# Attention over pairs of heads on one core: an earlier swap of the first query's rotary halves, and new orders of a pair's four blocks on three engines

## What is computed

```python
def _L0_attn_ref(x, W_kvd, b_kvd, W_ku, b_ku, W_vu, b_vu, W_kr, b_kr, W_qd, b_qd, W_qu, b_qu, W_qr, b_qr, W_o, b_o):
    ...
    kv_c = x @ W_kvd + b_kvd
    keys_c = heads(kv_c @ W_ku + b_ku, HD)
    values = heads(kv_c @ W_vu + b_vu, HD)
    keys_r = _apply_rope(heads(kv_c @ W_kr + b_kr, RD))
    q_c = x @ W_qd + b_qd
    queries_c = heads(q_c @ W_qu + b_qu, HD)
    queries_r = _apply_rope(heads(q_c @ W_qr + b_qr, RD))
    ...
    scores = jnp.einsum('bhqd,bhkd->bhqk', q, k) * scale
    scores = jnp.where(causal[None, None], jnp.float32(-1000000000.0), scores)
    probs = jax.nn.softmax(scores, axis=-1)
    ctx = jnp.einsum('bhqk,bhkd->bhqd', probs, values)
    ...
xn = _layernorm(x, axis=-1)
x = x + attn(xn) + einsum('bsi,oi->bso', xn, binarized(weight)) + bias
```

## Time and profile before

| what | value |
|---|---|
| median of 3 runs | 1412.74 us (1407.88 to 1415.17) |
| the profiled execution | 1410.69 us, span in the trace 1408.9 us |
| TensorE matmuls, share of the span | 97% |
| ScalarE | 85% |
| VectorE | 81% |
| GpSimd | 71% |
| mean granted TensorE clock | 0.997 of full speed |

### The profile page before, as it was taken

How to read it: one execution, slowest core, us unless ns; L and a number is a source line. 1 busy time by engine, 2 the same in 40 slices (tenths; PEclk the granted TensorE clock), 3 DMA queues, 4 the chain that set the end, 5 groups by cost and what they waited for, 6 DMA issues and landing times.

```text
span 1408.9 us, 27603 instructions
## 1 busy us (share of the span) xinstructions
PE 1373.1 (97%) x9786; PEld 1229.7 (87%) x9786; DVE 1146.4 (81%) x2708; ACT 1200.5 (85%) x2603; POOL 1000.4 (71%) x573
## 2 busy tenths in 40 slices
PE   6979999999999999999999999999999999999998
PEld 4769999997898999888899999999789999999987
DVE  4858898885788888887688889888678888888898
ACT  4659889997788988998788999899878988889887
POOL 6986777777667777769666787777766877777750
PEclk9999999999999999999999999999999999999999
DMA  9851222212343322211333222222233322221110
GB/s 274 228 127 50 72 54 64 64 50 64 76 107 79 83 64 64 64 34 47 79 94 92 64 80 64 65 57 57 63 77 87 88 64 65 64 60 45 40 31 31
DMA packets 46957, 106.82 MB, mean 76 GB/s; under 512 B 9333, under 2 KB 17830, under 8 KB 46822
## 3 DMA queue, kind: packets, MB, share of 16 engines
q1 hardware_dynamic: 43360, 94.01, 26.0%
q0 software_dynamic: 3296, 11.01, 2.8%
q10 hardware_dynamic: 166, 0.03, 0.0%
HBM read 48.92 MB, written 9.96 MB: 42 GB/s over the span
## 4 chain that ended last, share of the span: by engine, by line
PE 79%; ACT 7%; POOL 5%; DVE 5%; DMA 2%; issue 1%; SPq 1%; POOLq 0%; ACTq 0%; DVEq 0%
PE ring L1509 11%; PE turn L1564 10%; PE u_ps L1585 9%; PE ring L1539 9%; PE ring L1540 8%; PE ring L1541 8%; PE u_ps L1586 8%; PE o_ps L1609 4%; PE o_ps L1610 4%; PE ring L1522 3%; ACT probs L788 2%; PE ring L1448 2%; PE ring L1454 2%; DVE probs L1086 1%; DVE probs_lo L1096 1%; POOL k_rope L377 1%
## 5 line engine op out<-in xcount | busy, mean ns | idle before, releaser
L1086 DVE TENSOR_SCALAR_CACHE_REDUCE probs<-ring,c_t 128x1024 f32<-128x1024 f32 (+7 forms) x512 | 413.2, 809 | 85.7 <-PE ring L1541 85.2
L1096 DVE TENSOR_TENSOR probs_lo<-turn,probs_hi 128x512 fp32r<-128x512 f32 (+1 forms) x640 | 401.0, 630 | 65.7 <-ACT probs_hi L797 61.0
L797 ACT ACTIVATE probs_hi<-turn 128x512 fp32r<-128x512 f32 (+1 forms) x640 | 346.4, 550 | 94.0 <-PE turn L1564 91.2
L788 ACT ACTIVATE probs<-probs,row_min 128x1024 f32<-128x1024 f32 (+7 forms) x512 | 394.5, 772 | 11.8 <-DVE probs L1086 9.5
L1564 PE MATMUL turn<-ident,probs_r 128*128 128x128 f32 x2304 | 315.9, 244 | 4.6 <-DVE probs_lo L1096 2.7
L1585 PE MATMUL u_ps<-probs_hi,kv_nat 128*128 128x256 f32 x1147 | 313.5, 301 | 1.2 <-DVE u_pair L1102 1.2
L1564 PEld LDWEIGHTS turn<-ident,probs_r 128*128 128x128 f32 x2304 | 267.9, 141 | 36.5 <-DVE probs_lo L1096 15.3
L1586 PE MATMUL u_ps<-probs_lo,kv_nat 128*128 128x256 f32 x1147 | 289.7, 281 | 0.0
L1539 PE MATMUL ring<-k_hi,q_hi 128*128 128x512 f32 (+3 forms) x768 | 273.6, 356 | 0.0
L1540 PE MATMUL ring<-k_lo,q_hi 128*128 128x512 f32 (+3 forms) x768 | 262.9, 342 | 0.0
L1541 PE MATMUL ring<-k_hi,q_lo 128*128 128x512 f32 (+3 forms) x768 | 262.7, 342 | 0.0
(11 more groups left out here) (229 smaller groups left out, 2585.8 us busy)
## 6 DMA issues: line engine op xcount, KB each, us to landing
swapped<-k_rope SPq DMA_DIRECT2D x128, 128.0 KB, 2.3
wv<-wv_scratch SPq DMA_DIRECT2D x62, 256.0 KB, 4.0
wp<-wp_scratch SPq DMA_DIRECT2D x62, 192.0 KB, 3.5
wp<-wp_scratch SPq DMA_DIRECT2D x31, 256.0 KB, 3.1
swapped<-q_y SPq DMA_DIRECT2D x62, 128.0 KB, 2.3
swapped<-q_x SPq DMA_DIRECT2D x62, 128.0 KB, 2.3
k_hi<-qb_kv_hi SPq DMA_DIRECT2D x16, 256.0 KB, 3.7
k_lo<-qb_kv_lo SPq DMA_DIRECT2D x16, 256.0 KB, 5.0
```

The lines of the kernel that those rows point to most:

```text
L788: act.activation(p, p, ACT.Exp, scale=-1.0, bias=row_min[:, r:r + 1], accum_out=row_sum[:, g % 4, w, h:h + 1]).then_inc(exp_ready, 1)
L797: act.activation(probs_hi[:, r % 4, 0:width], turn[r % 2][:, 0:width], ACT.Identity).then_inc(turned_hi, 1)
L1086: dve.tensor_scalar(probs_of(g, w, h), ring[slot_of(entry)][:, KEY_COLUMN[qt]:KEY_COLUMN[qt] + keys], c_t[b % 2][:, qt, ds(pair * 2 + h, 1 ...
L1096: dve.tensor_tensor(probs_lo[:, r % 4, 0:width], turn[r % 2][:, 0:width], probs_hi[:, r % 4, 0:width].bitcast(F32), ALU.subtract).then_inc ...
```

## The change

The swap of a pair's queries is split. `swap(m, 1)` waited until both queries were evacuated and then issued the second query's two DMAs and the first's. Now it waits for the first query alone, issues its two DMAs, then waits for the second query and issues the other two; the keys, the first and the second query each signal a semaphore of their own, and `rope` waits for the first query's at its step 3 and for the second's at step 4.

Masks are calls of their own and no longer stand inside a group of transposes. The last score of block 3 of a pair (`scores(g - 1, 3, 0)`) stands at the beginning of the next pair's block 0, its exponential too. All four blocks have new orders on TensorE, ScalarE and VectorE, and two entries of `NEXT_BATCH` move. No computing instruction is added or removed.

```diff
-NEXT_BATCH = {(5, 3, 0): (("transpose", 0),), (5, 3, 3): (("transpose", 1),), (6, 0, 3): (("down", 0),), (6, 1, 2): (("down", 1),),
-              (6, 2, 2): (("linear", 0),), (6, 3, 2): (("linear", 1),), (7, 3, 0): (("natural", 0),), (7, 3, 2): (("natural", 1),)}
+NEXT_BATCH = {(5, 2, 3): (("transpose", 0),),
...
+              (6, 3, 0): (("linear", 0),),
...
-                    engine.wait_ge(swap_done, swaps_done(m, 0) if m > 0 else 16 * SWAP_DMAS)
-                if n == 3 and m > 0:
-                    engine.wait_ge(swap_done, swaps_done(m, 1))
+                    engine.wait_ge(keys_swapped, 16 * SWAP_DMAS * (m + 1))
+                if n in (3, 4) and m > 0:
+                    engine.wait_ge((x_swapped, y_swapped)[n - 3], 16 * 2 * m)
...
                 else:
-                    sp.wait_ge(evacuated, m * PROJ_ITEMS + PROJ_ITEMS)
+                    sp.wait_ge(evacuated, m * PROJ_ITEMS + QUERY_X + 1)
 
                     sp.wait_ge(rope_step, m * ROPE_OPS + 3)
...
+                    swap_rows(64, q_x, x_swapped)
+                    sp.wait_ge(evacuated, m * PROJ_ITEMS + QUERY_Y + 1)
+                    swap_rows(0, q_y, y_swapped)
+                    return
+                swap_rows(0, k_rope, keys_swapped)
+                swap_rows(64, k_rope, keys_swapped)
```

ScalarE's new order of block 0 (the lines that are new or stand elsewhere have a +):

```diff
                     evacuate(g, ROPE_K)
                     turned_high(g - 1, 0)
-                    u_again(g - 2, 0)
                     u_high(g - 2, 1)
                     turned_high(g - 1, 1)
+                    u_again(g - 2, 0)
+                    exponent(g - 1, 3)
+                    if pair == 5:
+                        next_apply(b + 1, 1)
+                    u_again(g - 2, 1)
+                    turned_high(g - 1, 2)
+                    exponent(g, 0)
+                    exponent(g, 1)
+                    turned_high(g - 1, 3)
+                    turned_high(g - 1, 4)
+                    u_high(g - 1, 0)
+                    exponent(g, 2)
                     if pair == 4:
                         next_inverse(b + 1)
-                    turned_high(g - 1, 2)
-                    if pair == 5:
-                        next_apply(b + 1, 1)
-                    turned_high(g - 1, 3)
-                    exponent(g, 0)
-                    exponent(g, 1)
-                    u_high(g - 1, 0)
-                    u_again(g - 2, 1)
-                    exponent(g, 2)
-                    turned_high(g - 1, 4)
-                    u_again(g - 1, 0)
+                    evacuate(g, QUERY_X)
                     if pair == 6:
                         next_left("down", b + 1, 0)
-                    evacuate(g, QUERY_X)
                     turned_high(g, 0)
+                    u_again(g - 1, 0)
                     turned_high(g, 1)
```

TensorE's of the same block:

```diff
                 if n == 0:
+                    scores(g - 1, 3, 0)
                     project(g, ROPE_K)
                     output(g - 3, 1)
+                    weigh_group(g - 2, 3)
                     turn_group(g - 1, 0)
-                    turn_group(g - 1, 1, (g, 0))
-                    weigh_group(g - 2, 3)
+                    turn_group(g - 1, 1)
+                    mask(g, 0)
                     weigh_group(g - 2, 4)
                     head_ready(g, 0)
                     scores(g, 0, 0)
                     scores(g, 0, 1)
-                    turn_group(g - 1, 2, (g, 1))
+                    turn_group(g - 1, 2)
+                    mask(g, 1)
                     output(g - 2, 0)
                     weigh_group(g - 1, 0)
+                    scores(g, 1, 0)
                     weigh_group(g - 1, 1)
-                    scores(g, 1, 0)
-                    turn_group(g - 1, 3, (g, 2))
+                    turn_group(g - 1, 3)
+                    mask(g, 2)
...
                     output(g - 2, 1)
-                    turn_group(g, 0, (g, 3))
+                    turn_group(g, 0)
+                    mask(g, 3)
+                    scores(g, 3, 0)
                     weigh_group(g - 1, 3)
-                    scores(g, 3, 0)
-                    turn_group(g, 1, (g + 1, 0))
+                    turn_group(g, 1)
+                    mask(g + 1, 0)
```

In block 1 two masks now stand between other matmuls, in block 3 one; the output of block 3 stands behind the second score there:

```diff
                     output(g - 2, 0)
-                    turn_group(g - 1, 2, (g, 1))
+                    mask(g, 1)
                     weigh_group(g - 2, 4)
...
                     weigh_group(g - 1, 0)
+                    mask(g, 3)
+                    scores(g, 3, 0)
+                    output(g - 2, 1)
                     weigh_group(g - 1, 1)
-                    turn_group(g - 1, 4, (g, 3))
-                    output(g - 2, 1)
-                    scores(g, 3, 0)
+                    turn_group(g - 1, 4)
...
+                    mask(g, 1)
                     scores(g, 1, 0)
+                    output(g - 2, 0)
...
+                    mask(g, 2)
+                    weigh_group(g - 1, 0)
                     scores(g, 2, 0)
```

More of the change, by code:

```diff
@@ L392, in _, with swap_rows @@
         def _(sp):
+            def swap_rows(rows, source, signal):
+                for a, b in ((rows, rows + 32), (rows + 32, rows)):
+                    sp.dma_start(swapped[a:a + 32, :], source[b:b + 32, :]).then_inc(signal, 16)
             def swap(m, which):
@@ L400, in swap @@
                 else:
-                    sp.wait_ge(evacuated, m * PROJ_ITEMS + PROJ_ITEMS)
+                    sp.wait_ge(evacuated, m * PROJ_ITEMS + QUERY_X + 1)
                     sp.wait_ge(rope_step, m * ROPE_OPS + 3)
-                for rows, source in ((0, k_rope if which == 0 else q_y), (64, k_rope if which == 0 else q_x)):
-                    for a, b in ((rows, rows + 32), (rows + 32, rows)):
-                        sp.dma_start(swapped[a:a + 32, :], source[b:b + 32, :]).then_inc(swap_done, 16)
+                    swap_rows(64, q_x, x_swapped)
[4 more added lines that the diff above has]
+                swap_rows(64, k_rope, keys_swapped)
             def load_wp(m):
@@ L865, in sequence @@
                     u_high(g - 1, 1)
                     turned_high(g, 1)
-                    if not (pair == 6 and b + 1 < NB):
-                        turned_high(g, 2)
-                elif n == 2:
+                    turned_high(g, 2)
+                else:
                     exponent(g, 0)
-                    if pair == 6 and b + 1 < NB:
-                        turned_high(g - 1, 2)
-                    turned_high(g - 1, 3)
+                    high_queries(g, 1)
                     u_again(g - 2, 1)
```

229 lines of the change are left out of this document (119 added, 110 removed).

## The result

The changed kernel takes 1399.35 us (median of 4 runs, 1398.56 to 1401.42) against 1412.08 for the kernel before on the same chips: a ratio of 0.9914, 95% interval 0.9886 to 0.9942. The profiled execution took 1401.42 us, its span is 1399.4. Batches are counted from 0 here and in the expectations, so the prediction's second batch is batch 1.

What follows compares the result with a forecast made beforehand. TensorE's list of matmuls was taken to bound the kernel, with 1.17 us of short waits per plain pair. 5.2 - 13.9 - 5.4 - 0.8 - 1.8 = -16.7 us gave a forecast of 1395 us, range 1382 to 1416.

Steps and rivals of the forecast that it cites:

- Positions: TensorE's new order, mainly three masks per pair between other matmuls at 0.12 us: +0.18 a plain pair, +5.2 in all.
- The waits: TensorE's short waits for ScalarE and VectorE: 1.17 us falls to 0.35 per plain pair, -13.9 over seventeen pairs.
- the prediction's margins: Time in hand in a plain pair: 0.2 us at the transposes, 0.45 at the mask behind the first query.
- the slower rival: Key projection waits for VectorE's minimum once 0.4 us in hand is used up: up to 1428 us, chance 0.12.
- the 38.25 worked out: Length in us of a plain pair in the new order if TensorE's matmuls had nothing to wait for.
- the better case: Rival: the five tight places hold, or lone masks cost no more: 1384 us, chance 0.10.
- the two steps of ScalarE that the prediction singled out: Fourth exponential moved three steps behind, first query's evacuation moved earlier: TensorE's waits of 0.15 and 0.23 us go.
- Pair 5: Pair also preparing the next batch: waits fall from 1.8 to 0.95 us in each of three batches.
- Pair 6: New 1.65 us mask wait behind the "down" evacuation, most other waits gone: -0.8 us over three pairs.
- The swap: First query's DMAs issued earlier: rotary chain ends about 3.6 us earlier, buying nothing in a plain pair.
- pair 0's -1.8: Gain from the earlier swap in the second batch's pair 0, where ScalarE waited for GpSimd: -1.8 us.
- First pair: With last pair and drain, has waits the order hardly touches: 0, give or take 1.5 us.

Runs made afterwards that it cites:

- experiment 7: Changed kernel with ScalarE's fourth exponential of the block before put back ahead of the keys' evacuation: 1432.80 us, ratio 1.0164 to the kernel before.
- experiment 11: Changed kernel with ScalarE's first query evacuation put back behind the block's first high halves and a copy: 1440.00 us, ratio 1.0196 to the kernel before.
- experiment 4: Changed kernel with ScalarE taking pair 6's first down projection out of the ring before evacuating the first query: 1396.37 us, ratio 0.9903 to the kernel before.
- experiment 2: Kernel before with the split swap alone, all orders as before: 1418.52 us, ratio 1.0063 to the kernel before.
- experiment 1: Changed kernel with the queries' swap late again, both behind the second query's evacuation: 1406.05 us, ratio 0.9976 to the kernel before.
- experiment 8: Changed kernel with the queries' swap late and ScalarE's high halves of the queries two steps later: 1394.26 us, ratio 0.9887 to the kernel before.
- experiment 3: Changed kernel with GpSimd's first query product in pair 0 waiting for VectorE's low half of the values: 1392.99 us, ratio 0.9883 to the kernel before.
- experiment 12: Changed kernel with GpSimd behind the values, pair 6's down projection first, a store behind the keys' swap: 1382.81 us, ratio 0.9805 to the kernel before.
- experiment 9: Changed kernel with GpSimd behind the values, down projection first, pair 0's second query evacuation ahead of keys' high halves: 1391.34 us, ratio 0.9867 to the kernel before.

## Why the prediction held, and where it failed

The direction, the range and the mechanism of the orders were right; the gain was 12.7 us instead of 17. That it came so near is in part luck: in the table, terms that came out worse than forecast add up to some 14 us and terms that came out better to some 7.

*Positions.* A lone mask costs the 0.12 that was taken from the earlier trace rows. The Trainium skill, TensorE: Matmul & The Clock Gate, The mechanism, would have it cost nothing extra; the rows of the mask above decide otherwise.

*The waits.* What TensorE's weight loads waited for the named causes, over the whole run (us in total, times, longest us), before and now:

```profile
PEld turn L1564 <- DVE probs_lo L1096: 15.3, 36, 0.7
PEld turn L1564 <- ACT probs L788: 7.1, 29, 0.9
PEld ring L1522 <- ACT q_x L702: 3.8, 23, 0.2
...
PEld turn L1571 <- DVE probs_lo L1103: 3.0, 8, 1.0
PEld turn L1571 <- ACT probs L799: 3.6, 5, 1.8
```

The mask's wait for the first query is gone altogether. Two of the places in a plain pair, the transposes behind the first two scores and the mask behind the first query:

```profile
1159.54 0.69 DVE L1103 TENSOR_TENSOR probs_lo<-turn,probs_hi 128x512 fp32r<-128x512 f32 x1
...
1160.80 0.28 PE L1571 MATMUL turn<-ident,probs_r 128*128 128x128 f32 x2
...
1167.80 1.12 ACT L713 ACTIVATE q_x<-ring,bias_p 128x1024 f32<-128x1024 f32 x1 [0.36 <-PE ring L1516]
...
1169.61 0.23 PE L1529 MATMUL ring<-mask_bf,ident_bf 128*128 128x128 bf16 x1
```

The low halves end 0.57 us ahead of the transposes and the evacuation 0.69 ahead of the mask. So the prediction's margins were too small: some 0.5 and 0.6 us are in hand, not 0.2 and 0.45. The key projection that was to wait in the slower rival hardly does: 0.17 us in three plain pairs. 0.24 us are left on the 38.25 worked out, where 0.35 were allowed for: a third of the way from the forecast to the better case. (That rival's terms, all taken, come to 1381 and not to its 1384.) Experiments 7 and 11 show that the two steps of ScalarE that the prediction singled out are needed: each, put back alone, costs 1.2 us a plain pair, more than the 0.75 gained. How the 0.75 divides among the moves is not shown. Pair 5 (-4.0, not -2.0) and pair 7 (-1.0, not +0.5) were undersized too, and pair 4 oversized (-1.4, not -2.3).

*Pair 6.* A wait of 1.65 behind the "down" evacuation was forecast; 1.44 stand in the trace, and experiment 4 takes it away.

GpSimd's waits in a plain pair became what was forecast (the second was to be about 1 us):

```profile
1174.50 2.40 POOL L380 TENSOR_TENSOR q_x<-q_x,cos 64x1024 f32<-64x1024 f32 x1 [0.17 <-POOL k_lo L391]
1177.65 2.39 POOL L380 TENSOR_TENSOR q_y<-q_y,cos 64x1024 f32<-64x1024 f32 x1 [0.75 <-DMA swapped<-q_y]
```

*The swap* is the step that failed, in both halves. "In a plain pair that buys nothing" was read from the old orders, for which experiment 2 shows it true; in the new ones it is worth some 0.6 us in a plain pair (experiment 1), because ScalarE's high halves of the queries had moved ahead, which I had laid out without asking when GpSimd delivers them (experiment 8). And pair 0's -1.8 became a loss: batch 1 did fall, by 1.4, but in the other batches GpSimd's product, no longer held up, lies on VectorE's split of the values. I asked what waits for GpSimd's product and not what runs beside it. Experiments 2 and 3 show this from both sides. A part of the loss is the keys' late swap, which experiment 12 takes away.

*First pair.* Taken as 0, it lost 3.0, by the same collision: 41.99 with GpSimd behind the values. The mean granted clock of this pair was 0.85, before 0.92, so the lower level lasted some 14 us there instead of 7.

Open: in the changed kernel GpSimd began 8.0 us after the keys' evacuation in batch 2, 2.0 more than the usual 4.35 and the late start of 1.67 explain (of the swap's four DMAs the third landed at 5.2 us, the last at 7.9); and why the clock stands at its lower level for part of some prologues. The three traces with the longest ones (39.66, 38.27 and 37.27 us, of experiments 4, 11 and 9) have 10.2, 3.4 and 3.4 us of it; this blurs medians of 4 to 6 runs.

## What to carry to other kernels

When a step of one engine starts earlier, lay it beside what every other engine does in its new place, not only beside its readers: an idle stretch that is filled may have been what a neighbour's instruction ran in. Work that happens once per batch (a store, a split of values) meets an order that was laid out for plain steps; look at each queue's list at that boundary. The steps of an order hang together: two of them put back alone (experiments 7 and 11) each cost more than the whole change had gained, while a third (4) took away a wait that the prediction had priced, and gave 4.8 us in its trace. So look at each moved step against its neighbours on every engine.

## What the hardware showed that was not expected

VectorE's subtraction of two SBUF tiles (128x512) takes 0.69 us alone and, where it finds a GpSimd product running, ends about 0.55 us after that, 2.5 to 2.8 in all. It is the second to begin that pays: in experiment 4's batch 1 VectorE began 0.16 us ahead and took 0.69, and GpSimd's product took 2.79 instead of 2.40:

```profile
431.56 0.69 DVE L1080 TENSOR_TENSOR kv_nat<-xn,kv_nat 128x512 fp32r<-128x512 f32 x1
431.72 2.79 POOL L380 TENSOR_TENSOR q_x<-q_x,cos 64x1024 f32<-64x1024 f32 x1 [0.68 <-DMA swapped<-q_x]
```

A subtraction of VectorE that reads PSUM ran beside such a product without that (0.68 for 128x512 at 1097.95, under the product that GpSimd began at 1097.71).

And a wait of 1.8 us on TensorE was followed, 1.6 us after its end, by 3.4 us at the clock's lower level: in pair 0 of batch 3 the wait is 1.8 of the 3.5 us by which the pair exceeds 38.49, and most of the rest are matmuls at that level (256 columns every 0.21 us instead of 0.12).
